# A state-space scan in eight cores: two state products in one VectorE instruction

## The reference

```python
xz = einsum('bld,de->ble', layernorm(x), in_proj_w)      # d_inner = 2048
x_, z = split(xz, 2)                                     # x_: causal conv of 4 taps, then silu
bcd = einsum('ble,ep->blp', x_, x_proj_w)                # B (16), C (16), one dt
dt = softplus(bcd[..., -1:] * dt_w + dt_b)
dA  = exp(dt[..., None] * A)                             # 16 states for each channel
dBx = (dt * x_)[..., None] * B[:, :, None, :]
h = dA_t * h + dBx_t ;  y_t = sum_n h * C_t              # over all 2048 positions
y = (y + x_ * D) * silu(z);  x = x + layernorm(y @ out_proj_w)
# then: one shared MLP and 15 experts, all computed densely, weighted by top-3 router probabilities
x = x + layernorm(shared + routed)
```

## Time and profile before

| | |
|---|---|
| time, median of two runs | 8109.92 us (7985.16 and 8234.67) |
| the profiled execution | 8052.77 us |
| span of its slowest core (core 3) | 8051.2 us |
| spans of all cores | 7949.3 to 8051.2 us |
| busy PE / DVE / ACT | 3237.3 / 3598.9 / 2014.6 us |
| busy PEld / POOL | 1287.0 / 187.4 us |
| chain that ended last, by engine | PE 33%, DVE 29%, DMA 18%, ACT 8% |

### The profile page before, as it was taken

One profiled execution on the slowest core, in us unless ns is written; L12 is line 12 of the kernel. 1 busy time (PEld: TensorE's weight loads), 2 busy tenths in 40 slices (PEclk: granted clock), 3 DMA queues, 4 the chain that ended last, 5 costly groups with the idle time before them and its releaser, 6 DMA issues.

```text
span 8051.2 us, 48655 instructions; the slowest of 8 cores (7949.3 to 8051.2 us)
## 1 busy us (share of the span) xinstructions
PE 3237.3 (40%) x11876; PEld 1287.0 (16%) x11876; DVE 3598.9 (45%) x5513; ACT 2014.6 (25%) x2925; POOL 187.4 (2%) x380
## 2 busy tenths in 40 slices
PE   0010220002334555553335555543345555547776
PEld 0000110001111222221112222211112222212222
DVE  0000128893226676742236767722256777621112
ACT  2000133332123333321133333211233333221111
POOL 0302000000000000000000000000000000000000
PEclk9999855555556777775557777765566777767776
DMA  5799500001111222221102222111111221212222
GB/s 160 113 119 118 79 28 4 3 3 34 47 35 42 63 63 63 63 59 47 56 11 63 63 63 63 59 43 47 45 34 61 63 62 59 58 41 84 84 84 68
DMA packets 428598, 474.08 MB, mean 59 GB/s; under 512 B 52079, under 2 KB 416881, under 8 KB 423169
## 3 DMA queue, kind: packets, MB, share of 16 engines
q1 hardware_dynamic: 402850, 366.09, 15.5%
q0 software_dynamic: 25472, 104.88, 8.8%
HBM read 521.10 MB, written 88.08 MB: 76 GB/s over the span
## 4 chain that ended last, share of the span: by engine, by line
PE 33%; DVE 29%; DMA 18%; ACT 8%; issue 7%; SPq 3%; DVEq 1%; POOL 0%; ACTq 0%; POOLq 0%
DVE h_buf L1187 15%; PE p_proj L699 14%; DMA w_kt<-scr_in 11%; PE p_proj L640 11%; DVE m_dbx L1183 5%; PE p_proj L906 4%; DMA f_wb<-scr_e 3%; SPq L596 2%; DVE conv_acc L966 2%; DMA w_kt<-scr_out 1%; DVE h_buf L1194 1%; PE p_proj L1292 1%; DMA cast_stage<-w_out 1%; ACT L662 1%; DMA scr_in<-cast_bf 1%
## 5 line engine op out<-in xcount | busy, mean ns | idle before, releaser
L640 PE MATMUL p_proj<-f_xln,f_wb 128*128 128x512 bf16 x4096 | 1187.1, 462 | 1363.4 <-ACT f_he L662 961.1
L1155 ACT ACTIVATE m_da<-m_dtg,k_a 128x512 f16<-128x512 f16 x1024 | 731.8, 720 | 2170.5 <-DVE h_buf L1187 2160.3
L699 PE MATMUL p_proj<-f_he,f_wb 128*128 128x512 bf16 x4096 | 1091.0, 434 | 317.5 <-DMA f_wb<-scr_e 309.3
L1187 DVE TENSOR_TENSOR_SCAN h_buf<-m_da,h_last,m_dbx 128x512 f16<-128x512 f16 x768 | 985.4, 1283 | 82.8 <-DVE m_dbx L1183 3.7
L737 DVE TENSOR_TENSOR y_tmp<-p_proj,f_cwrep 128x512 f16<-128x512 f32 x480 | 332.0, 692 | 1294.8 <-PE p_proj L699 1197.8
L906 PE MATMUL p_proj<-m_xln,w_kt 128*128 128x256 bf16 x2048 | 492.0, 410 | 990.1 <-DMA w_kt<-scr_in 784.9
L640 PEld LDWEIGHTS p_proj<-f_xln,f_wb 128*128 128x128 bf16 x4096 | 458.5, 114 | 2090.2 <-issue 1875.8
L961 DVE TENSOR_SCALAR conv_acc<-u_pre,k_conv_w 128x256 f16<-128x256 bf16 x128 | 35.8, 280 | 1414.7 <-ACT u_pre L933 739.0
L699 PEld LDWEIGHTS p_proj<-f_he,f_wb 128*128 128x128 bf16 x4096 | 434.9, 108 | 944.9 <-issue 674.4
L1183 DVE TENSOR_TENSOR m_dbx<-m_wdt,brep 128x512 f16<-128x512 f16 x1024 | 435.5, 425 | 112.3 <-DVE h_buf L1187 3.2
L1292 PE MATMUL p_proj<-z_s,w_kt 128*128 128x512 bf16 x512 | 167.9, 466 | 728.0 <-DVE z_s L1217 643.7
(11 more groups left out here) (146 smaller groups left out, 2247.6 us busy)
## 6 DMA issues: line engine op xcount, KB each, us to landing
f_wb<-scr_e SPq DMA_DIRECT2D x2048, 128.0 KB, 2.5
w_kt<-scr_in SPq DMA_DIRECT2D x512, 128.0 KB, 2.0
scr_e<-e_w POOLq DMA_DIRECT2D x240, 256.0 KB, 141.3
cast_stage<-w_in POOLq DMA_DIRECT2D x8, 2048.0 KB, 10.4
w_kt<-scr_out SPq DMA_DIRECT2D x128, 128.0 KB, 2.0
scr_in<-cast_bf SPq DMA_DIRECT2D x64, 128.0 KB
cast_stage<-w_out POOLq DMA_DIRECT2D x16, 512.0 KB, 4.6
out<-f_out POOLq DMA_DIRECT2D x32, 256.0 KB, 2.6
```

Of the source, the lines that this page charges most:

```text
L640: inst = t_.matmul(p_proj[:, j * TF:(j + 1) * TF], f_wb[:, hs, k % 4, (hmg * 2 + j) * 128:(hmg * 2 + j + 1) * 128], f_xln2[:, k, :], start ...
L699: inst = t_.matmul(p_proj[:, 1024 + j * TF:1024 + (j + 1) * TF], f_wb[:, hsC if k < 4 else hsD, k % 4, (dmg * 2 + j) * 128:(dmg * 2 + j + ...
L1155: s.activation(m_da[:, dpar, :], m_dtg[:], ACT.Exp, scale=k_a[:, g_, n:n + 1]))
L1187: v.tensor_tensor_scan(h_buf[:, n, :], m_da[:, dpar, :], m_dbx[:], init, AL.mult, AL.add))
```

## The change

m_dbx gets a second slot of 512 columns, and one VectorE product makes the inputs of two scans: m_wdt is read twice (a broadcast over a new middle dimension) and multiplied by brep[:, n:n+2, :]. It is issued for even n; the scan of odd n waits for its Exp and for the scan before it, and reads the second half. Sixteen products of 512 columns in a group become eight of 1024. The scans, the Exp and everything after them stay as they are. m_spt, which had the size of the slot that m_dbx gains, is dropped: Exp writes m_dtg and Ln works in place, and for that the Exp of group g (g >= 1) waits as well for the last state's Exp of group g-1. The token counts follow.

```diff
-            m_spt = msb("m_spt", (128, SC), F16)
-            m_dbx = msb("m_dbx", (128, SC), F16)
+            m_dbx = msb("m_dbx", (128, 2, SC), F16)
...
                         if g_ >= 1:
                             s.wait_ge(c_v.h, tk[("wdt", sc_i, g_ - 1)])
-                        t1 = c_s.inc(s.activation(m_spt[:], m_dtr[:], ACT.Exp,
+                            s.wait_ge(c_s.h, tk[("da", sc_i, g_ * NS - 1)])
+                        t1 = c_s.inc(s.activation(m_dtg[:], m_dtr[:], ACT.Exp,
...
-                            s.activation(m_dtg[:], m_spt[:], ACT.Ln, bias=1.0))
+                            s.activation(m_dtg[:], m_dtg[:], ACT.Ln, bias=1.0))
...
                             v.wait_ge(c_s.h, tk[("da", sc_i, i)])
-                            if n == 0:
-                                v.wait_ge(c_v.h, tk[("wdt", sc_i, g_)])
+                            if n % 2 == 0:
+                                if n == 0:
+                                    v.wait_ge(c_v.h, tk[("wdt", sc_i, g_)])
+                                else:
+                                    v.wait_ge(c_v.h, tk[("scan", sc_i, i - 1)])
+                                if g_ == 0 and n == 0:
+                                    v.wait_ge(c_s.h, tk[("crep", sc_i, NS - 1)])
+                                bcast = m_wdt[:].unsqueeze(1).broadcast_to((128, 2, SC))
+                                assert tk[("dbx", sc_i, i)] == c_v.inc(
+                                    v.tensor_mul(m_dbx[:], bcast, brep[:, n:n + 2, :]))
+                                v.wait_ge(c_v.h, tk[("dbx", sc_i, i)])
                             else:
                                 v.wait_ge(c_v.h, tk[("scan", sc_i, i - 1)])
-                            assert tk[("dbx", sc_i, i)] == c_v.inc(
-                                v.tensor_mul(m_dbx[:], m_wdt[:], brep[:, n, :]))
-                            v.wait_ge(c_v.h, tk[("dbx", sc_i, i)])
                             init = 0.0 if sc_i == 0 else h_last[:, g_, n:n + 1]
                             assert tk[("scan", sc_i, i)] == c_v.inc(
                                 v.tensor_tensor_scan(h_buf[:, n, :], m_da[:, dpar, :],
-                                                     m_dbx[:], init, AL.mult, AL.add))
+                                                     m_dbx[:, n % 2, :], init,
+                                                     AL.mult, AL.add))
```

More of the change, by code:

```diff
@@ L1122, in build_program @@
                     tk[("wdt", sc_i, k_)] = _pos + 1
[L1123 to L1128, removed]
+                    for pp in range(NS // 2):
+                        tk[("dbx", sc_i, k_ * NS + 2 * pp)] = _pos + 2 + 3 * pp
+                        tk[("scan", sc_i, k_ * NS + 2 * pp)] = _pos + 3 + 3 * pp
+                        tk[("scan", sc_i, k_ * NS + 2 * pp + 1)] = _pos + 4 + 3 * pp
+                    tk[("hcp", sc_i, k_)] = _pos + 26
+                    tk[("yg", sc_i, k_)] = _pos + 37
+                    _pos += 37
                 if _t is not None:
@@ L1175, in f @@
                             v.wait_ge(c_s.h, tk[("da", sc_i, i)])
-                            if n == 0:
-                                v.wait_ge(c_v.h, tk[("wdt", sc_i, g_)])
+                            if n % 2 == 0:
[9 more added lines that the diff above has]
+                                v.wait_ge(c_v.h, tk[("dbx", sc_i, i)])
                             else:
                                 v.wait_ge(c_v.h, tk[("scan", sc_i, i - 1)])
-                            if g_ == 0 and n == 0:
-                                v.wait_ge(c_s.h, tk[("crep", sc_i, NS - 1)])
-                            assert tk[("dbx", sc_i, i)] == c_v.inc(
-                                v.tensor_mul(m_dbx[:], m_wdt[:], brep[:, n, :]))
-                            v.wait_ge(c_v.h, tk[("dbx", sc_i, i)])
                             init = 0.0 if sc_i == 0 else h_last[:, g_, n:n + 1]
```

## The result

The changed kernel runs in 7848.87 us, the median of 11 runs (7827.72 to 7975.44), against 8111.79 us for the kernel before (10 runs). The ratio is 0.9798 with a 95% interval of 0.9762 to 0.9833: 2.0% faster, so just at the border of what counts as faster, where 1.5% had been forecast. Of 8053 us that is 163 us in place of 123.

The account below looks back on a forecast made before the run. VectorE was taken to pace the first super-chunk, and VectorE and TensorE to alternate in interleaved stages, with the path through the last Exp. 8052.77 - 33.9 - 89.0 = 7930 us, range 7845 to 8070.

Parts of the forecast that it names:

- the sum: Whole kernel: the profiled 8052.77 us less 33.9 and 89.0 us gives 7930 us; chance 0.57.
- The product's price: Paired m_dbx product on VectorE: 0.692 us for 1024 columns, taken from L1206, with no penalty for the repeated operand.
- The slow operand: Rival at L1183: the repeated operand makes the product 1.226 us, +125 us, 8178 us in all; chance 0.07.
- The pair's saving: VectorE's products and scans: two states take 3.58 us in place of 3.84, saving 0.265 us a pair.
- Seven pairs in the interleaved groups, eight in the first super-chunk: Pairs on the path in each group: eight in the first super-chunk save 33.9 us, seven in interleaved groups 89.0 us.
- the eighth pair: Interleaved groups, behind the fourteenth scan: only lengthens VectorE's idle; if it counted, another 12.7 us.
- The sign that the prediction named for that: VectorE's wait before the first L737 of a group: longer, not shorter, by about 0.26 us.
- The shared buffer and the Exp's margins at no cost: ScalarE: the new wait on m_dtg is hidden and states' Exp are not late, state 2's 0.56 us early; cost 0.
- the term of 89.0 us for the interleaved turns: Super-chunks 1 to 3: 7 pairs, 16 groups, 3 super-chunks, 336 x 0.265 = 89.0 us saved.
- turns as quick as the best one: Rival, interleaved w1 turns: half of 48 run like the best, 62 us more saved, 7868 us; chance 0.20.
- The other rival of the clock: Interleaved w1 turns: half run like the five at 72.0 us, 86 us come back, 8016 us; chance 0.10.

Follow-up runs that it names:

- the four legs of the table: Changed kernel with m_wdt issued once, three or five times (+0, +1.06, +2.13 us), and kernel before (+1.86): turns 65.14, 66.86, 67.78 and 67.65 us.
- the last kernel: Changed kernel with four slots of m_da, 42 unread matmuls before w1's second part and 16 before w2: 7658.74 us, ratio to before 0.9476.

## Why the prediction was right, and where it was short

The forecast was 7930 us in 7845 to 8070, within 2% with chance 0.70. The measured 7848.87 us lies in that range, 4 us above its lower edge, and the ratio, 2.0% with an interval of 1.7 to 2.4%, lies on the border between the two classes. That it fell on the inner side of both is partly luck. Of the 81 us between forecast and result, about half is the starting point: by the ratio the kernel before stands at 7848.87 / 0.9798 = 8011 us, 42 us under the 8052.77 that the sum started from, an execution in which cores 0 to 3 lost clock as shown above. The other 39 us are saving that the sum did not have.

*The product's price* was right to the nanosecond: 692 ns. The slow operand, 1.226 us, did not happen. By the rule in Vector Engine (DVE) Microarchitecture Reference, section 5.1, of the Trainium skill, a row read again and again keeps two elements a cycle, and this trace agrees with its 692 ns at 1024 columns.

*The pair's saving* of 0.265 us was right: 3.58 us in place of 3.84, and 2.13 us a group in the first super-chunk.

*Seven pairs in the interleaved groups, eight in the first super-chunk* was right. The leg from w2's end to the next 48 matmuls went, by median, from 32.07, 31.73 and 31.72 us in the three stages to 29.89, 29.90 and 29.90, which is 1.8 to 2.2 against 1.86; the eighth pair is not in it. The sign that the prediction named for that, VectorE's idle before its first take-in longer by 0.26 us, did not come: in the mean of 45 turns the idle went from 10.51 to 10.31 us. The 48 matmuls in front of that take-in had become 0.49 us shorter, and 0.26 - 0.49 = -0.23 is close to the -0.20 measured, so the eighth pair does lie in the idle time, but this reading leans on the shorter burst. Four slots of m_da then moved the turn by the two scans and one product that the same argument gives.

*The shared buffer and the Exp's margins at no cost* were right: 1.0014 with the buffer alone, and no wait for an Exp between the scans.

*The step that was short* is the term of 89.0 us for the interleaved turns. It took TensorE's bursts as fixed blocks. They are not: in the 45 turns of core 6 before and core 0 after, the leg went from a mean of 31.81 to 29.95 us, the 48 matmuls from 12.73 to 12.24, the transfer between the bursts stayed at 6.57, and w2 went from 16.55 to 16.37. The bursts give 0.67 us and the leg 1.86, together the 2.5 us by which the turn shrank, 48 x 2.51 = 120 us in place of 89. Adding length to the leg took it back, and keeping TensorE busy took it out of the comparison. The prediction had the clock among its rivals, with turns as quick as the best one giving 7868 us, and took it for chance from one execution to the next. It was an answer to the change itself: the paired kernels' cores have turns of 65.10 to 65.56 us in two executions, those with single products 67.43 to 68.13 in three, wherever the clock was not lowered. That bursts are no fixed blocks could be seen before: the kernel before has turns of 66.0 to 68.5 us on core 6, past the first two of each stage, with bursts of 12.0 to 13.1 us, at the same leg. The other rival of the clock, turns of 72 us as in the five of the earlier trace rows, was a different thing: on core 3 these lie where the granted clock was 0.81, as in the burst of core 0 shown above.

*Its size could not have been read beforehand* as exactly: the burst is 12.1 us with four slots, at a leg 3.55 us shorter than the changed kernel's, and 12.0, 13.0, 12.8 and 12.7 us at the four legs of the table, so its direction at the next leg does not follow from its direction at the last.

What stays open: 18.2 us were saved outside the turns and the first super-chunk's groups, of which three legs and the sixteenth group make 7.7. By the rows of w1's starts they fall 4.2 before the first turn, 7.8 and 4.2 between the stages and 1.9 behind the last; the stage ends were not taken further apart. Open too is how a leg fixes the number of matmuls that run at the low clock. The 1.94 us a turn that 42 unread matmuls brought in the kernel with two slots are not open: the 48 matmuls gave 1.73 in the mean, the transfer 0.12 and w2 0.11.

## What to carry to other kernels

When instructions wait for each other one by one, two of them made into one save a fixed cost and a gap, here 159 + 107 ns, and the elements still cost the same; count only those that lie before the point where the path leaves the engine. Look for that point first: here it was the last Exp, and two more slots in front of it were worth 3.55 us a turn, more than the whole change. And where TensorE works in bursts between long waits, a burst's length depends on the wait in front of it, so a saving in the wait can come out a third larger (2.51 us for 1.86 here), or smaller (0.92 us for 1.07 between the two longer legs).

## What the runs showed of the hardware

An operand with a repeated row of 512 f16 columns costs the two-operand product nothing: 692 ns for 1024 columns, with or without it.

A burst of the same 48 matmuls took 10.5, 12.0, 12.8 or 13.3 us, by what TensorE did before it: 10.5 us right behind other matmuls, the rest after idling for 15 to 20 us. Behind an idle stretch the first 7 to 13 matmuls of 512 columns start 0.427 us apart, at a granted clock of 0.50 (1.2 GHz), and the others 0.216 us apart at 1.00 (2.4 GHz). The length of the idle time alone does not tell how many: 12.1 us after 14.97, 11.98 after 16.85, 12.62 after 18.44, 13.25 after 19.62, 12.82 after 20.39.

Some cores have stretches at a third granted clock, 0.81, in which a dense burst takes 266 ns a matmul in place of 219. They come to the cores of a die in pairs. In the last kernel's execution and in that of the kernel before, cores 0 and 1 had them first and cores 2 and 3 later, without overlap in time, and cores 4 to 7 had none; in that of the changed kernel cores 4 and 5 had them between 3121 and 6847 us, cores 6 and 7 between 4162 and 7888, mostly in turn, and cores 0 to 3 none.

The Trainium skill, TensorE: Matmul & The Clock Gate, Part 1, tells of a limiter that passes 13 of 16 clock pulses once three cores of a die run dense matmuls, and takes the whole die there. By its figure 216 ns would become 266 (an estimate), and the traces agree with that and, 13/16 being 0.81, with the granted clock. They do not show it for the whole die at once: over the stage in which cores 0 and 1 had 0.75, core 2 had 0.89.
